# Banded attention: reordered copies and their stores move to ScalarE, with one semaphore per part, and the projections and outputs are spread over a group

## The reference

```python
OFFSETS = sorted(set(range(0, 33)) | {48, 64, 96, 128, 192, 256, 384})
qkv = x @ Wqkv + bqkv                 # x is layer-normed; 16 heads of 16
scores[.., i] = q . shift(k, OFFSETS[i]) * scale + pos_bias[i]   # -inf before the first token
alpha = softmax(scores)               # over the 40 offsets
out = sum_i alpha[i] * shift(v, OFFSETS[i])
x = x + (out * sigmoid(x @ Wgate + bgate)) @ Wout + bout
```

## Time and profile before

| | us |
|---|---|
| median of 3 runs | 4303.57 (4297.05 to 4304.6) |
| the profiled execution | 4299.21 |
| its span | 4297.2 |
| banded attention, of it | about 2052 (88 to 2140) |
| one batch of it, from group 0's end to the next one's | 244 to 252 |
| PE busy in the span | 3077.0 (72%) |

### The profile page before, as it was taken

One profiled execution on the slowest core, in us unless ns is written; L12 is line 12 of the kernel. 1 busy time (PEld: TensorE's weight loads), 2 busy tenths in 40 slices (PEclk: granted clock), 3 DMA queues, 4 the chain that ended last, 5 costly groups with the idle time before them and its releaser, 6 DMA issues. The chain is left out here.

```text
span 4297.2 us, 99681 instructions
## 1 busy us (share of the span) xinstructions
PE 3077.0 (72%) x45340; PEld 1777.4 (41%) x45340; DVE 1704.4 (40%) x2814; ACT 1168.6 (27%) x1262; POOL 691.6 (16%) x491
## 2 busy tenths in 40 slices
PE   1264646556464665647689848998999989998898
PEld 0143434434343443435434524444444444443345
DVE  4032322222222322222350446666666666664502
ACT  0011111111111111111131015454545545455310
POOL 0302222210222222121000012121211212120000
PEclk9577767777676777867789769999999999999897
DMA  4434444254444424444129332222322223220295
GB/s 115 108 78 92 99 92 100 59 112 87 102 90 91 107 52 112 87 112 100 32 89 412 132 72 56 45 60 53 65 48 46 60 53 68 46 60 5 89 413 206
DMA packets 232386, 419.63 MB, mean 98 GB/s; under 512 B 112922, under 2 KB 141412, under 8 KB 215588
## 3 DMA queue, kind: packets, MB, share of 16 engines
q1 hardware_dynamic: 219796, 410.68, 36.4%
q10 hardware_dynamic: 12176, 2.66, 0.5%
HBM read 316.49 MB, written 94.40 MB: 96 GB/s over the span
## 5 line engine op out<-in xcount | busy, mean ns | idle before, releaser
L1339 DVE TENSOR_REDUCE b_tops<-b_slot 128x8 f32<-128x1024 f32 x576 | 680.5, 1220 | 358.0 <-PE b_slot L1196 179.0
L1376 ACT ACTIVATE b_probs<-b_slot 128x1024 f32<-128x1024 f32 x576 | 582.4, 1022 | 553.5 <-PE b_slot L1196 397.7
L570 PE MATMUL a_slot<-a_bias_q,a_ident 128*128 128x512 bf16 x256 | 108.5, 518 | 340.4 <-DMA a_k_stack<-orders_dram 278.4
L1216 PE MATMUL b_outT_ps<-b_probs,b_v 128*17 128x128 f32 (+3 forms) x4608 | 320.8, 386 | 6.1 <-ACT b_probs L1376 5.5
L745 DVE TENSOR_REDUCE a_tops<-a_slot 128x16 f32<-128x1024 f32 x128 | 156.5, 1223 | 389.3 <-PE a_slot L550 387.7
L1196 PE MATMUL b_slot<-b_q_stack,b_k_stack 99*128 99x512 bf16 (+3 forms) x1280 | 274.3, 321 | 44.0 <-DVE b_tops L1339 32.8
L1196 PE MATMUL b_slot<-b_k_stack,b_q_stack 96*128 96x512 bf16 (+3 forms) x1280 | 265.3, 322 | 29.4 <-DVE b_tops L1339 20.6
L1143 POOL TENSOR_SCALAR_AFFINE_SELECT b_probs<-b_probs 128x1024 f32<-128x1024 f32 x128 | 139.6, 1091 | 812.2 <-ACT b_probs L1376 812.2
L736 DVE TENSOR_TENSOR a_probs<-a_slot,a_bias_k 128x1024 f32<-128x1024 f32 x128 | 154.9, 1218 | 242.2 <-PE a_slot L550 241.9
L606 PE MATMUL a_outT_ps<-a_probs,a_v_near 128*17 128x64 f32 (+1 forms) x8448 | 178.9, 257 | 99.3 <-issue 98.6
L793 ACT ACTIVATE a_row_home<-a_slot 12x1024 bf16<-12x1024 f32 x32 | 32.5, 1014 | 791.1 <-PE a_slot L589 791.1
(11 more groups left out here) (217 smaller groups left out, 4661.9 us busy)
## 6 DMA issues: line engine op xcount, KB each, us to landing
f_w_ring<-in_L_ffn_w_dram SPq DMA_DIRECT2D x128, 1024.0 KB, 9.9
orders_dram<-a_parts SPq DMA_DIRECT2D x96, 512.0 KB
a_k_stack<-orders_dram SPq DMA_DIRECT2D x128, 256.0 KB, 7.6
a_q_stack<-orders_dram SPq DMA_DIRECT2D x64, 384.0 KB, 5.8
parts_dram<-b_parts SPq DMA_DIRECT2D x96, 256.0 KB
a_q_stack<-orders_dram SPq DMA_DIRECT2D x64, 256.0 KB, 5.8
a_k_stack<-orders_dram SPq DMA_DIRECT2D x128, 128.0 KB, 9.1
b_k_stack<-parts_dram SPq DMA_DIRECT2D x64, 256.0 KB, 6.9
```

The lines of the kernel that those rows point to most:

```text
L1216: ins = pe.matmul(outT_ps[32 * h:32 * h + HD + 1, first:last], v1[b % 2][:, j, HG * g + h, :], src[:, base + first:base + last], start=u = ...
L1339: ins = dve.tensor_reduce(out, src, AX.X, ALU.max)
L1376: act.activation(probs_of(b, g, u, h)[:, :], slot_of(step)[:, :], ACT.Exp).then_inc(taken_act, 1)
```

## The change

- `turn` becomes three steps, `turn0`, `turn1`, `turn2`, done by ACT and not by POOL, each as soon as its part is there. Behind each, ACT waits for its own copy and then issues the store of that part itself. SP stores no parts any more.
- The semaphore of the stores becomes three, one per part; so `part0`, `part1` and `part2` of the next projection each wait for the store of their own part alone.
- The DRAM buffer of the parts has room for two batches, so a store waits for the loads of two batches ago.
- `fillers` gives each group six places (five between or behind the S and mx and the near PV, and one behind `ote`), with one projection per place. The division of a projection is no longer a block behind it: its seven steps are dealt out one or two at a time behind S, mx, v, zt, ot and the PV numbered 3 and 7.
- `ote` comes ahead of the work that is placed behind the PV. The second gate, one `at` and one `op` come at the end of group 0, the second pair in group 1, and the gate waits for `gmul`.
- In groups 0 and 2 the load of the second next operand buffer comes behind `mrow`, in the far PV, and no longer behind the last S.

```diff
-    def projections(b, half):
-        out = []
-        for which in "qk":
-            out += [(which, b, half)] + [(step, b, half, which) for step in ("part0", "rest1", "part1", "part2", "turn", "spill")]
-        return out
+
+    def division(which, b, half):
+        return [(step, b, half, which) for step in ("part0", "rest1", "turn0", "part1", "part2", "turn1", "turn2")]
+
+    def projection(which, b, half):
+        return [(which, b, half)] + division(which, b, half)
...
+    def fillers(b, g):
+
+
+        more, earlier = b < B - 1, b > 0
         if g == 0:
-            first = [("ot", b - 1, 3), ("gmul", b - 1), ("at", b - 1, 0), ("op", b - 1, 0), ("at", b - 1, 1), ("op", b - 1, 1)] if b else []
-            return first, [("gate", b, 0), ("gate", b, 1)]
-        first, last = [("ot", b, g - 1)], []
-        if g == 1 and b:
-            last += [("stats", b - 1, i4) for i4 in range(2)]
-        if b < B - 1:
-            if g == 1:
-                first += [("z", b + 1, 0), ("zt", b + 1, 0), ("z", b + 1, 1), ("zt", b + 1, 1)]
-            if g in (1, 3):
-                p = projections(b + 1, g // 2)
-                last = p + last if g == 1 else last
-                first = first + p[0:7] if g == 3 else first
-                last = p[7:] if g == 3 else last
-            if g == 2:
-                v = values(b + 1)
-                first += v[0:2]
-                last += v[2:4]
-        return first, last
-
-    seq = [("z", 0, 0), ("zt", 0, 0), ("z", 0, 1), ("zt", 0, 1)] + projections(0, 0)
-    seq += operands(0) + operands(1) + operands(2) + projections(0, 1) + values(0)
-    seq += [("mx", 0, 0, h) for h in range(HG)] + [("fparts", 0, 0), ("fp", 0, 0), ("mred", 0, 0), ("mt", 0, 0), ("mrow", 0, 0)]
+            return ([("ot", b - 1, 3), ("gmul", b - 1)] if earlier else [], [], [], [("gate", b, 0)], [],
+                    ([("at", b - 1, 0)] if earlier else []) + [("gate", b, 1)] + ([("op", b - 1, 0)] if earlier else []))
+        if g == 1:
+            return ([("at", b - 1, 1)] if earlier else [], [("op", b - 1, 1)] if earlier else [],
+                    [("ot", b, 0)] + ([("z", b + 1, 0)] if more else []), [("zt", b + 1, 0), ("z", b + 1, 1)] if more else [],
+                    [("zt", b + 1, 1)] if more else [],
+                    ([("q", b + 1, 0)] if more else []) + ([("stats", b - 1, i4) for i4 in range(2)] if earlier else []))
+        if g == 2:
+            return [], [("k", b + 1, 0)] if more else [], [("ot", b, 1)], [("v", b + 1, 0), ("vout", b + 1, 0)] if more else [], [], \
+                [("q", b + 1, 1)] if more else []
+        return [], [("ot", b, 2)], [], [("v", b + 1, 1), ("vout", b + 1, 1)] if more else [], [], [("k", b + 1, 1)] if more else []
...
-            cuts = [len(first) * k // 3 for k in range(4)]
-            seq += [("vin", b, g), ("S", b, g, 0)] + tops[0] + [("S", b, g, 1)] + operands(n + 3) + tops[1]
-            seq += first[cuts[0]:cuts[1]] + [("S", b, g, 2)] + first[cuts[1]:cuts[2]] + [("S", b, g, 3)] + operands(n + 4)
-            seq += first[cuts[2]:cuts[3]] + tops[2] + tops[3] + ([("fparts",) + after] if more else [])
-            seq += near + ([("fp",) + after, ("mred",) + after] if more else [])
-            seq += far[0:4] + ([("mt",) + after, ("mrow",) + after] if more else []) + far[4:8]
-            seq += last + [("ote", b, g)]
+
+            late = g in (0, 2)
+            seq += [("vin", b, g), ("S", b, g, 0)] + place[0] + top[0] + [("S", b, g, 1)] + operands(n + 3) + place[1] + top[1]
+            seq += [("S", b, g, 2)] + place[2] + [("S", b, g, 3)] + ([] if late else operands(n + 4)) + top[2] + place[3] + top[3]
+            seq += ([("fparts",) + after] if more else []) + near + place[4] + ([("fp",) + after, ("mred",) + after] if more else [])
+            seq += far[0:4] + ([("mt",) + after, ("mrow",) + after] if more else []) + (operands(n + 4) if late else [])
+            seq += far[4:8] + [("ote", b, g)] + place[5]
...
+    out, waiting = first, []
+    for step in seq:
+        out.append(step)
+        if step[0] in "qk":
+            out += waiting
+            waiting = division(*step)
+        elif waiting and (step[0] in ("S", "mx", "v", "zt", "ot") or step[0] == "PV" and step[4] in (3, 7)):
+
+            upto = 2 if waiting[0][0] in ("part0", "part1") else 1
+            out += waiting[:upto]
+            waiting = waiting[upto:]
+    return out + waiting
...
+                        hold(pool, spilled[2], 16 * (count("part2", *step) - 1))
                         pool.tensor_tensor(parts[:, 2, 0, :], full, parts[:, 1, 0, :], ALU.subtract).then_inc(part2_done, 1)
-                    elif kind == "turn":
-                        _, b, half, which = step
-
-                        pool.wait_ge(part2_done, count("part2", "part2", b, half, which))
-                        for part in range(PARTS):
-                            pool.tensor_copy(parts[:, part, 1, :].rearrange("p (r a) -> p r a", r=LINKS),
-                                             parts[:, part, 0, :].rearrange("p (a r) -> p r a", r=LINKS)).then_inc(turned, 1)
...
-                    if kind == "spill":
-                        _, b, half, which = step
-                        m = "qk".index(which)
-                        sp.wait_ge(turned, PARTS * count("turn", "turn", b, half, which))
-                        if b:
-
-                            for g, pair in ((2 * half, 0), (2 * half, 1), (2 * half + 1, 0), (2 * half + 1, 1)):
-                                n = ring(b - 1, g, pair)
-                                sp.wait_ge(stacked[n], STACK * count(f"stack{n}", "stack", b - 1, g, pair))
-                        for part in range(PARTS):
-                            sp.dma_start(scratch["orders"].ap()[m, half, :, part], parts[:, part, :, :]).then_inc(spilled, 16)
-                    elif kind == "stack":
+                    if kind == "stack":
                         _, b, g, pair = step
                         n = ring(b, g, pair)
-                        sp.wait_ge(spilled, SPILL * count("spill", "spill", b, g // 2, "k"))
+                        for part in range(PARTS):
+                            sp.wait_ge(spilled[part], 16 * count(f"turn{part}", f"turn{part}", b, g // 2, "k"))
...
-                        hold(act, spilled, SPILL * (count("part0", *step) - 1))
+                        hold(act, spilled[0], 16 * (count("part0", *step) - 1))
                         act.activation(parts[:, 0, 0, :], full, ACT.Copy).then_inc(part0_done, 1)
                     elif kind == "part1":
                         _, b, half, which = step
                         act.wait_ge(rest1_done, count("rest1", "rest1", b, half, which))
+
+                        hold(act, spilled[1], 16 * (count("part1", *step) - 1))
                         act.activation(parts[:, 1, 0, :], full, ACT.Copy).then_inc(part1_done, 1)
+                    elif kind in ("turn0", "turn1", "turn2"):
+                        _, b, half, which = step
+                        part, m = int(kind[-1]), "qk".index(which)
+                        if part == 2:
+                            act.wait_ge(part2_done, count("part2", "part2", b, half, which))
+                        else:
+                            act.wait_ge((part0_done, part1_done)[part], count(f"part{part}", f"part{part}", b, half, which))
+
+                        act.activation(parts[:, part, 1, :].rearrange("p (r a) -> p r a", r=LINKS),
+                                       parts[:, part, 0, :].rearrange("p (a r) -> p r a", r=LINKS), ACT.Copy).then_inc(turned, 1)
+                        act.wait_ge(turned, PARTS * (count("turn2", "turn2", b, half, which) - 1) + part + 1)
+                        if b >= 2:
+
+                            for g, pair in ((2 * half, 0), (2 * half, 1), (2 * half + 1, 0), (2 * half + 1, 1)):
+                                n = ring(b - 2, g, pair)
+                                act.wait_ge(stacked[n], STACK * count(f"stack{n}", "stack", b - 2, g, pair))
+                        act.dma_start(scratch["orders"].ap()[b % 2, m, half, :, part], parts[:, part, :, :]).then_inc(spilled[part], 16)
...
+                            if b and not i4:
+                                act.wait_ge(gmul_done, count("gmul", "gmul", b - 1))
...
-    scratch["orders"] = nc.dram_tensor("orders_dram", [2, 2, 8, PARTS, HD, 2, N], BF16)
+    scratch["orders"] = nc.dram_tensor("orders_dram", [2, 2, 2, 8, PARTS, HD, 2, N], BF16)
```

More of the change, by code:

```diff
@@ new lines, in fillers @@
+        return [], [("ot", b, 2)], [], [("v", b + 1, 1), ("vout", b + 1, 1)] if more else [], [], [("k", b + 1, 1)] if more else []
+    first = [("z", 0, 0), ("zt", 0, 0), ("z", 0, 1), ("zt", 0, 1)] + projection("q", 0, 0) + projection("k", 0, 0)
+    first += operands(0) + operands(1) + operands(2) + projection("q", 0, 1) + projection("k", 0, 1)
+    first += [step for i4 in range(2) for step in (("v", 0, i4), ("vout", 0, i4))]
```

(28 more changed lines are left out.)

5 lines of the change are left out of this document (1 added, 4 removed).

## The result

The changed kernel takes 3870.42 us (median of 4 runs, 3860.39 to 3881.03) against 4304.09 us: the ratio is 0.8989, with a 95% interval of 0.8951 to 0.9026. The forecast was 3940 us, in a range of 3830 to 4130. So the direction and the range held, and the gain was 434 us where 364 were forecast (359 from the profiled execution). The profiled execution took 3860.39 us, its span 3858.7.

What follows compares the result with a forecast made beforehand. PE sets the pace but idles behind queues held up in order. From the profiled 4299.2 us: seven batches (248.4 to 203.4) -315, ahead of the first group -50, first group 0 -4, last batch +4: 3934, called 3940; range 3830 to 4130.

Steps and rivals of the forecast that it cites:

- rival 1: All batches: waits get shorter still, clock more often full, issue gaps overlap; batch 187 us, 3820 in all; chance 15%.
- Operand loads: PE's waits for operand loads, with stores off SP's queue: from 34.3 to 17 us per batch.
- ote: PE's wait for `ote` on ACT, with `ote` ahead of the division: from 19.5 to about 1 us per batch.
- Group 2: Both projections of a half are divided there; PE newly waits some 6 us for a PSUM slot until k is copied.
- the walk: Group 2 stepped through from the end of q's matmuls: k's copy at 14.4 us, last exponential 24.7, PE at PV 25.5.
- Spreading: Projections and outputs spread among other PE work: PE's small waits for DVE and ACT from 21.5 to about 20 us per batch.
- Clock: PE's granted clock rises from 0.74 to 0.78 with its busy share: busy time from 147 to 139 us per batch.
- Gaps: PE's issue gaps inside the PV: left at 26.4 us per batch, 15 gaps of 1.8 us, as the instructions are the same.
- Rival 4: PE starved of instructions inside the PV: each gap 6 us, batch 266 us, 4375 in all; chance 5%.
- ACT: Turned copies 1.06 us and issues 1.34 us each, 29 us per batch on ACT, just hidden by PE's work in group 2.
- Ahead of the first group: Four divisions before PE's first S, about 12 us each, not 25: 50 us saved, with ends 30 and 65.
- The rival of contention: Stores running beside loads make operand waits, gaps and lost clock larger: batch 222 us, 4074 in all; chance 20%.

Runs made afterwards that it cites:

- e_ote_first: The kernel before with one edit, `ote` placed ahead of the work behind the PV: 4303.75 us, against 4304.09 for the kernel before.
- e_load_early: The changed kernel with the late operand load of groups 0 and 2 moved from behind `mrow` to ahead of fp: 3864.37 us, against 3870.42.
- e_stores_sp: The changed kernel with the stores and their wait for the copy moved from ACT to SP, at the same places: 4032.52 us, against 3870.42.
- e_load_early_g2: The changed kernel with the late operand load moved ahead of fp in group 2 only: 3851.31 us, against 3874.21 for the changed kernel run again.

## Why the prediction held, and where it was off

The stated range held. The measured 3870 lies 5 us below the narrower one that was given to the forecast itself (3875 to 4015, batch 195 to 215), nearer to rival 1's batch of 187 than to 203.4. So it held by its outer bounds, with several terms off in both directions.

- **Operand loads**: 34.3 to 17 forecast, 21.0 measured. The places were right: per batch 5.1 in group 0 (5 forecast), 2.4 in group 1 (2; nearly all in the first batch), none in group 2 (0). The miss is group 3, with two waits of 6.8 us on the mean, 13.6 for 10.
- **ote**: 19.5 to 1 forecast, 0 measured. The number came right for the wrong reason. I booked it as a saving beside that of the loads; e_ote_first shows that alone it is worth nothing. What made the sum come out is that the change removes the common cause of both.
- **Group 2**: the walk had DVE's copy of k 14.4 us from the end of q's matmuls; it came 14.1 us after that of q began, which is where q's matmuls ended. PE's new wait was put at 6 us and was 2.5 + 1.9 in the group shown (2 + 3 on the mean); PE's projection of k ran 6.66 us there and not 3.6, where q's same 8 matmuls just before it had run 3.70.
- **Spreading** is the term that was most mis-sized: 21.5 to 20 forecast, 11.7 measured (57.0 us of idle per batch, less 21.0 for loads and 24.3 of gaps). Before, 122 us of waits, 17.4 per batch, made up most of it: 40.4 for z, 27.3 for gmul, 27.3 of S for a PSUM slot until DVE had copied a projection, 27.1 for ACT's copy in the output product. They went almost wholly; the new ones are 7. The lower end that I had given it was 12.
- **Clock**: busy time 147 to 139 forecast, 133.8 measured, of which 2 are the output product that moved. I had drawn a line through 0.61 at 30% and 0.74 at 59% busy; at 70% it was 0.84. Such a line is no rule: of two groups of one batch, one busy for 65% had 0.72 and the next, busy for 68%, had 0.82.
- **Gaps** were left at 26.4 and are 24.3. Rival 4 (6 us each) did not come, but its mechanism is what the gaps are (below), and it is real in small: e_load_early moved loads into the PV and 36 us of gaps came.
- **ACT**: copy 2.06 us (my upper end), issue 0.59 (below my lower end): 32 us per batch for 29. The cover held. The 1.34 us per issue on SP was a mean over unlike ones: of three stores in a row the first two took 0.64 and 0.62 us and the third 2.64 (medians of 32), and a store by itself takes SP 0.58 in e_stores_sp. So ACT is no quicker at it than SP.
- **Ahead of the first group**: the first S at 186.91 and not 233.45, 46.5 us for 50.

By terms, a batch is 57.6 us shorter and not 45: 9.8 - 1.5 = 8.3 more from spreading, 4.9 from PE's busy time, 2.1 from the gaps, 1 from `ote`, less 3.7 from the loads. Seven times 12.6 is 88 us. Of these 3.5 are given back ahead of the first group and 11 outside the seven batches: the first group 0 gained 9.4 us and not 4, the last batch from its marker on took 137.0 us and not 120.5, 16.5 more where I had put 4 (the second gate and the whole output product of the batch before now stand behind the marker), and the stages behind it took 3.9 more. That gives the profiled 3860.

Rival 1 had nearly the right size (batch 187), and gave a reason that was half right, the clock. The Trainium skill's rule on issuing engines (DMA: Bandwidth & Descriptors, section "Issuing engines are not separate DMA queues"), weighed in the prediction, would have left it near 4245. It names only the starting engine's own time, and this case does not agree: e_stores_sp shows 162 us for the issuing engine alone, in waits inside its stream. The rival of contention was too dear.

**What the gaps in the PV are.** The profile names no releaser for them, but the traces tell. Counted over PE's stream, matmuls and weight loads together, all 94 gaps of the kernel after stand at the same place of every 256 instructions (within one), and so do all 104 of the kernel before. In group 0 of the last batch 128 matmuls (and as many weight loads) lie between one gap and the next, then 32 + 8 + 88:

```profile
1552.00 1.88 PE L599 MATMUL a_outT_ps<-a_probs,a_v_near 128*17 128x64 f32 x128 [0.95 <-issue]
1555.74 0.59 PE L599 MATMUL a_outT_ps<-a_probs,a_v_near 128*17 128x64 f32 x32 [1.87 <-issue]
1556.26 0.41 PE L573 MATMUL a_slot<-a_far_parts,a_perm 128*128 128x64 bf16 x8
1556.60 0.96 PE L609 MATMUL a_outT_ps<-a_probs,a_v_far 128*17 128x32 f32 x88
1559.31 0.53 PE L609 MATMUL a_outT_ps<-a_probs,a_v_far 128*17 128x32 f32 x40 [1.75 <-issue]
```

The seven batches have 218 such places, and one DMA queue moved 218 packets of 16 KB of the kind "instruction" in them (number of packets, MB, share of the 16 engines):

```profile
q8 instruction: 218, 3.57, 1.2%
```

Each gap ends 1.2 to 1.6 us after such a packet has ended (median 1.4). So PE stands in them for its next 256 instructions; of the 114 places in the PV, 94 show it. The long ones come with traffic at that moment: in the 5 us before the packet's end, 178 GB/s for the 9 gaps of 3 us and more, 43 for the 74 under 2 us. And they follow the moved load: gaps of 3 us and more are 3 in group 2 and none in group 0 after, 8 and 6 in e_load_early, 9 and none in e_load_early_g2, while group 1, where nothing moved, has 6, 6 and 5. No run tried to shorten them.

## What to carry to other kernels

Two waits of an engine are two terms only if they have different causes: ask of each whether the engine, coming earlier, would only wait longer for the same landing. A transfer whose input is late should not be issued by a stream that carries others' transfers; the bandwidth may have room while the queue stands. And a serial chain wants both, to be dealt out between the engine's own urgent steps and to be shortened: here one half gave 121 us, the other 245, and both 434. For idle time that has no releaser, count the instructions between one gap and the next.

## What was not expected of the hardware

- A bf16 copy on ACT that reads every 16th element (L813) took 2.06 us for 128x1024, twice the 1.06 us of the rounding copy of the same size, and as long as on POOL (2.03).
- An issue of a 512 KB store took 0.59 us on ACT (median of 96) and 0.58 on SP in e_stores_sp (median), but 2.64 us when it was the third in a row on SP in the kernel before (median of 32).
- PE's gaps in stretches of short matmuls are waits for its instructions: one possible place in 256 instructions, 170 us in the seven batches.
